# A four-stage transformer-like kernel: sine tables in paced pieces, bias adds and last weights placed late, ones set by VectorE

## The reference

```python
x = x + tanh(g_xattn[0]) * mamba(ctx_1024, layernorm(x))       # selective scan
x = x + tanh(g_ffn[0])   * moe(layernorm(x))                   # 16 experts, top 2, plus a shared one
x = x + tanh(g_xattn[1]) * attention(layernorm(x), ctx_1024)   # below
x = x + tanh(g_ffn[1])   * ffn(layernorm(x))                   # ternary weights, int8-like rows

# attention: 32 heads of 16, queries from x, keys and values from the context
q, k = axial_rope(x @ Wq, pos), axial_rope(ctx @ Wk, pos)      # cos and sin of pos * freq
w = softmax(q @ k.T / 4)
out = (w @ (ctx @ Wv)) @ Wout + bout
# ffn: w_q = clip(round(w / rms(w)), -1, 1) * rms(w);  x_q = round(x * 127 / max|x|)
out = bitlinear(gelu(bitlinear(x, w1)), w2)
```

## Time and profile before

| what | value |
|---|---|
| median of 3 runs | 1558.94 us |
| lowest and highest | 1556.22 and 1568.86 us |
| the profiled execution's own time | 1561.57 us |
| its span, first to last instruction | 1559.7 us |
| mean granted TensorE clock in it | 0.964 of full speed |
| busy: TensorE, VectorE, ScalarE, GpSimd | 1431.7, 1110.9, 998.1, 657.7 us |

### The profile page before, as it was taken

How to read it: one execution, slowest core, us unless ns; L and a number is a source line. 1 busy time by engine, 2 the same in 40 slices (tenths; PEclk the granted TensorE clock), 3 DMA queues, 4 the chain that set the end, 5 groups by cost and what they waited for, 6 DMA issues and landing times. The chain is left out here.

```text
span 1559.7 us, 20801 instructions
## 1 busy us (share of the span) xinstructions
PE 1431.7 (92%) x6056; PEld 613.8 (39%) x6057; DVE 1110.9 (71%) x1628; ACT 998.1 (64%) x1544; POOL 657.7 (42%) x440
## 2 busy tenths in 40 slices
PE   6688988988988979999999899699999999999999
PEld 2344434434444424444444344123333333244444
DVE  7999999999996422222222488889999999647985
ACT  3999998999974003323233154478788788877764
POOL 0689799698986530056656565240000000000000
PEclk7799999999999989999999999699999999999999
DMA  5212314113205374779963566352322322220464
GB/s 189 68 52 83 95 55 121 42 56 109 75 15 197 141 143 108 195 194 247 313 175 95 196 202 163 101 182 75 96 74 73 95 76 73 61 108 14 88 142 122
DMA packets 181164, 183.46 MB, mean 118 GB/s; under 512 B 104564, under 2 KB 132596, under 8 KB 180324
## 3 DMA queue, kind: packets, MB, share of 16 engines
q1 hardware_dynamic: 113846, 123.83, 27.8%
q0 software_dynamic: 9472, 33.89, 7.6%
q10 hardware_dynamic: 57776, 24.89, 6.6%
HBM read 96.97 MB, written 54.92 MB: 97 GB/s over the span
## 5 line engine op out<-in xcount | busy, mean ns | idle before, releaser
L1924 DVE TENSOR_REDUCE a_mx<-a_s 128x2 f32<-128x1024 f32 x256 | 303.2, 1218 | 35.3 <-PE a_s L2041 32.4
L284 POOL TENSOR_TENSOR m_hs<-m_hs,m_C 128x1024 f32<-128x1024 f32 x128 | 301.6, 2376 | 54.3 <-DVE m_hs L509 53.5
L509 DVE TENSOR_TENSOR_SCAN m_hs<-m_dA,m_d 128x512 f32<-128x512 f32 x256 | 294.6, 1201 | 11.8 <-PE m_d L664 10.8
L1376 PE MATMUL e_gu<-e_w,e_xgT 128*128 x376 | 171.0, 598 | 5.9 <-issue 5.9
L664 PE MATMUL m_d<-ident_sb,m_dBuT 128*128 128x128 f32 x1024 | 160.7, 291 | 16.6 <-DVE m_hs L509 9.9
L390 ACT ACTIVATE m_dA<-m_dt,m_negA 128x512 f32<-128x512 f32 x256 | 167.9, 711 | 11.2 <-DMA m_dt<-m_dt 10.6
L664 PEld LDWEIGHTS m_d<-ident_sb,m_dBuT 128*128 128x128 f32 x1024 | 118.0, 146 | 141.0 <-DVE m_hs L509 72.0
L368 ACT ACTIVATE m_dBuT<-m_dtuT,m_BT 128x512 f32<-128x512 f32 x241 | 157.8, 711 | 0.4 <-PE m_d L664 0.3
L2041 PE MATMUL a_s<-ring_sb 96*128 96x512 bf16 x512 | 152.3, 390 | 5.9 <-DVE a_mx L1924 4.0
L679 PE MATMUL m_y<-m_hs,m_fold 128*64 128x512 f32 x512 | 142.2, 636 | 3.7 <-POOL m_hs L284 3.7
L2315 POOL MEMSET f_ones<- 128x128 f32 x1 | 0.2, 204 | 343.3 <-POOLq L1508 343.3
(11 more groups left out here) (350 smaller groups left out, 2404.3 us busy)
## 6 DMA issues: line engine op xcount, KB each, us to landing
e_w<-in_ex_gu SPq DMA_DIRECT2D x16, 1024.0 KB, 7.9
ring_sb<-qk_dram SPq DMA_DIRECT2D x64, 192.0 KB, 3.2
xg_dram<-zeros_sb SPq DMA_DIRECT2D x47, 256.0 KB, 3.1
yg_dram<-attn_sb ACTq DMA_DIRECT2D x47, 256.0 KB, 3.6
m_C<-c_dram SPq DMA_DIRECT2D x64, 128.0 KB, 2.9
m_dt<-m_dt SPq DMA_DIRECT2D x64, 128.0 KB, 2.4
e_w<-in_ex_dn SPq DMA_DIRECT2D x16, 512.0 KB, 9.9
ring_sb<-qk_dram SPq DMA_DIRECT2D x64, 128.0 KB, 3.2
```

Source lines behind the costliest of these rows:

```text
L284: pool.tensor_tensor(hs[:, J % RH], hs[:, J % RH], C2[:, N % RC].unsqueeze(1).broadcast_to([P, 2, L]), ALU.mult).then_inc(s_hc, 1)
L509: dve.tensor_tensor_scan(hs[:, J % RH, h], dA[:, j % RA], pd[j % RD][:], 0.0, ALU.mult, ALU.add)\
L1376: last = pe.matmul(pgu[par][:], lhs(k), rhs(k), start=(k == 0), stop=(k == KD - 1))
L1924: dve.tensor_reduce(mx[:, r % 2, h * TB + 2 * c:h * TB + 2 * c + 2], psc[c][:], AX.X, ALU.max)\
```

## The change

Four edits, each to where or when something is done; what is computed stays the same.

1. In `moe`, the 8 table loads no longer stand together behind the scatter. Load q waits for `s_y` = NT + 1 + q, and they are issued between the early loads, two behind each of the first four. The wait for all tables comes behind the first seven early loads, ahead of the first key rows.
2. In `attention`, GpSimd's 16 additions of the bias wait for the last split of maxima (`s_n` = 4 * NG).
3. The load of `w1` leaves GpSimd's queue. SyncE issues it in four pieces of 1 MB, one at the end of its part of each of the last four steps; SyncE waits for all stored parts between the first four steps and the loop. ScalarE waits for four pieces.
4. The memset of the ones in `vout` goes from GpSimd's to VectorE's queue, first in both.

```diff
--- before.py
+++ after.py
@@ -973,9 +973,6 @@
             pool.wait_ge(s_sct, 16 * 2 * NT)
             pool.wait_ge(s_tst, 16)
             pool.sem_inc(s_kd, 2)
-            for q in range(HALF):
-                pool.dma_start(tab[q * HD:(q + 1) * HD], tab_dram[:, q, :].partition_broadcast(HD)).then_inc(s_tab, 16)
-            pool.wait_ge(s_y, NT)
             at = {"ctxT": 0, "wv": KC * T, "wk": KC * T + KC * D, "wq": KC * T + 2 * KC * D}
 
             def load_early(n, name, k, width, col=0):
@@ -984,6 +981,10 @@
                     pool.wait_ge(s_early, 16 * n)
                 to = at[name] + k * (T if name == "ctxT" else D) + col
                 pool.dma_start(early[:, to:to + width], a[name][k * P:(k + 1) * P, col:col + width]).then_inc(s_early, 16)
+
+            def load_table(q):
+                pool.wait_ge(s_y, NT + 1 + q)
+                pool.dma_start(tab[q * HD:(q + 1) * HD], tab_dram[:, q, :].partition_broadcast(HD)).then_inc(s_tab, 16)
 
             EARLY = [("wk", k, D) for k in range(KC)] + [("ctxT", k, L, b * L) for b in range(B) for k in range(KC)] + \
                 [("wv", k, D) for k in range(KC)] + [("wq", k, D) for k in range(KD)]
@@ -1014,11 +1015,15 @@
                     dst = qk_dram[1, m, :, c * HALF:(c + 1) * HALF].rearrange("a d h t -> (d h) a t")
                     pool.dma_start(dst, kparts[:, c]).then_inc(s_kst, 16)
 
-            pool.wait_ge(s_tab, 16 * HALF)
             for m in range(2 * B):
                 first = 0 if m == 0 else KEYS_FROM + 2 * m
                 for n in range(first, min(KEYS_FROM + 2 * m + 2, len(EARLY))):
                     load_early(n, *EARLY[n])
+                    if m == 0:
+                        for q in range(2 * n, min(2 * n + 2, HALF)):
+                            load_table(q)
+                if m == 0:
+                    pool.wait_ge(s_tab, 16 * HALF)
                 key_rows(m)
             pool.wait_ge(s_kst, 32 * 2 * B)
 
@@ -1680,6 +1685,12 @@
                 if inside(i, r + 1):
                     load_v(i, r + 1)
                     maxima(i, r + 1)
+                if isinstance(i, int) and i == NG // RG - 1:
+                    sp.dma_start(w1[:, r], a["w1T"][r * P:(r + 1) * P]).then_inc(s_last, 16)
+
+            def parts_stored():
+                for r in range(RP):
+                    sp.wait_ge(s_ps[r], 32 * ITEMS // RP)
 
             for b in range(B):
                 sp.wait_ge(s_vc, TB * (b + 1))
@@ -1705,14 +1716,13 @@
             for n in range(ITEMS - 2, ITEMS):
                 store(n)
 
-            run(sp, step)
+            run(sp, step, parts_stored)
             sp.wait_ge(s_t, 16 * (NG - 2))
             sp.dma_start(flat[:, half // 2:half // 2 + KD * D].rearrange("p (k e) -> p k e", k=KD),
                          a["wo"].rearrange("(k p) e -> p k e", p=P)).then_inc(s_wo, 16)
 
         @block.gpsimd
         def _(pool):
-            pool.memset(vout.rearrange("p r g t (h c) -> p (r g t h) c", h=G4)[:, :, HD:VW], 1.0).then_inc(s_vone, 1)
             pool.wait_ge(s_yst[0], 16 * (ST - ST // 2))
             pool.wait_ge(s_yst[1], 16 * (ST // 2))
             def inverse_root(b):
@@ -1753,13 +1763,11 @@
                 part_3(n - 1)
             part_3(ITEMS - 1)
             pool.dma_start(bo[:], a["bo"].partition_broadcast(P)).then_inc(s_bo, 16)
-            for r in range(RP):
-                pool.wait_ge(s_ps[r], 32 * ITEMS // RP)
-            pool.dma_start(w1[:], a["w1T"].rearrange("(k p) e -> p k e", p=P)).then_inc(s_last, 16)
             pool.wait_ge(s_bo, 16)
             pool.tensor_scalar(bo[:], bo[:], g_out, None, ALU.mult).then_inc(s_bg, 1)
             pool.wait_ge(s_bg, 1)
             pool.wait_ge(s_xn, NT)
+            pool.wait_ge(s_n, 4 * NG)
             for t in range(NT):
                 pool.tensor_tensor(x_sb[:, t], x_sb[:, t], bo[:], ALU.add).then_inc(s_xb, 1)
 
@@ -1874,6 +1882,7 @@
 
         @block.vector
         def _(dve):
+            dve.memset(vout.rearrange("p r g t (h c) -> p (r g t h) c", h=G4)[:, :, HD:VW], 1.0).then_inc(s_vone, 1)
             dve.memset(m3[:], 0.0).then_inc(s_zero, 1)
 
             def combine(t):
@@ -2324,11 +2333,11 @@
 
         @block.scalar
         def _(act):
-            weights = ((w1[:], w1q, s_w), (w2, w2q[:], s_w2))
+            weights = ((w1[:], w1q, s_w, 16 * KD), (w2, w2q[:], s_w2, 16))
 
             def square(n):
-                w, wq, loaded = weights[n]
-                act.wait_ge(loaded, 16)
+                w, wq, loaded, count = weights[n]
+                act.wait_ge(loaded, count)
                 act.activation(wq, w, ACT.Square, accum_out=ssq[:, n:n + 1]).then_inc(s_sq, 1)
 
             def weight_std(n):
@@ -2336,7 +2345,7 @@
                 act.activation(sd[:, n:n + 1], sd[:, n:n + 1], ACT.Sqrt).then_inc(s_sd, 1)
 
             def round_weight(n):
-                w, wq, loaded = weights[n]
+                w, wq = weights[n][:2]
                 act.wait_ge(s_k, 2 * n + 2)
                 act.wait_ge(s_c, 3)
                 act.activation(w, w, ACT.Identity, scale=rms[:, n:n + 1], bias=magic[:, 0:1]).then_inc(s_q, 1)
```

## The result

| | before | after |
|---|---|---|
| median, us | 1564.57 (1556.09 to 1569.64, 20 runs) | 1553.57 (1547.98 to 1566.45, 20 runs) |
| ratio to before, 95% interval | 1 | 0.9935 [0.9918, 0.9952] |
| span of the profiled execution, us | 1559.7 | 1551.6 |

The change takes 0.65% off, some 10 us (the ratio is taken over all runs; that of the two medians is 0.9930); the forecast was 0.73%, 11.3 us. The median of 1553.57 lies above the 1547.6 forecast mainly because before itself, in the twenty runs beside it, has a median of 1564.57 and not the 1558.94 of the three shown.

The account below looks back on a forecast made before the run. TensorE was taken to bound the kernel nearly throughout, with VectorE in the attention loop. The terms -7.5 + 1.0 - 4.8 + 0.2 - 0.2 sum to -11.3 us, forecasting 1547.6 us, range 1542 to 1555.

Parts of the forecast that it names:

- Tables: Behind the scatter: without the table burst, TensorE's 5.89 us stall and 1.57 us of slow products go, -7.5 us.
- The signs named for this part: At the first routed tile: transposes land under 7 us, no TensorE gap before it, eight first products in 3.6 us.
- The stall has no other owner: Behind the scatter: without the tables, turned rows arrive by 570, before TensorE's work ends at 578.32; 5.89 us of standing goes.
- Pieces: Routed experts: paced table pieces may delay turned rows near the first weight reload by up to 2.2 us each; +1.0 us.
- rival A: First transposed loads stay slow for another reason, such as two blocking each other; only -5 us, 1554 us; 12%.
- One sign of being wrong: Routed experts: ScalarE waits over 2 us for turned rows within the first ten tiles.
- Rival C: Slower: paced pieces fill the DMA engines beside the expert reload; 15.6 us lost against 12.5 gained, 1562 us; 5%.
- Additions and weights: Early attention loop: moving the bias additions and the 4 MB weight load away gives -4.8 us, bounds 2 and 5.3.
- Rival B: Long early attention steps belong to the loop's start, not to additions and weights; only -6.5 us, 1552.5 us; 12%.
- Weights late: End of attention: four pieces on SyncE's queue stay hidden, output weights land between 1365 and 1370; +0.2 us, bounds 0 and 1.5.
- additions at the end: Behind the last split: the sixteen additions end near 1371.3, covered by some 5 us; cost 0, bounds 0 to 1.
- Ones: Ahead of the gathers: memset moved to VectorE frees GpSimd's queue, gathers at most 0.8 us earlier; -0.2 us.

Follow-up runs that it names:

- e1: The kernel before with only the sine tables loaded in paced pieces; 1547.43 us, ratio 0.9926 to before.
- e6: The changed kernel itself, unaltered, run again beside the others; 1546.65 us, ratio 0.9918 to before.
- e5: The changed kernel with the eight table pieces started four tiles earlier, four of them ahead of the early loads; 1542.35 us, ratio 0.9900 to before.
- e9: The changed kernel with table pieces four tiles earlier and without the sixteen bias additions (output lacks the out bias); 1542.03 us, ratio 0.9892 to before.
- e4: The changed kernel with the tables loaded in one burst behind the scatter again; 1554.62 us, ratio 0.9965 to before.
- e2: The kernel before with only the sixteen bias additions moved behind the last split of maxima; 1556.16 us, ratio 0.9980 to before.
- e7: The changed kernel with all eight table pieces issued at once behind the first routed tile; 1554.36 us, ratio 0.9962 to before.
- e10: The changed kernel with table pieces four tiles earlier and the sixteen additions released at the 16th split of maxima; 1550.67 us, ratio 0.9938 to before.

## Why the prediction was right

**Tables, forecast -7.5.** The place, the owner and the size in the pair of profiles held: 6.4 us less from scatter to first routed product (26.48 to 20.05), and behind it 1.57 less for eight products. The signs named for this part came: first rows in 3.00 us, no gap, 3.60 us. What I mis-sized is what the burst costs in a usual execution. "The stall has no other owner" was true, but I took its 5.88 us for its price; it was the part of 11 us that the standstill of ScalarE and TensorE during the scatter had not already covered. A second profile of a kernel with the burst would have shown it.

**Pieces, forecast +1.0, bounds 0 and 7.** Measured: 2.0 us of gaps in after, 1.5 in e1, and in e6 two gaps of 4.4 and 4.3 us and a slow clock. Against e5's 286.6 us from the first routed product to attention that is 3.2 us in after, 2.6 in e1 and 14 in e6. The value was near in after, but the upper bound was too low. I priced a piece by what it takes of the DMA engines, 2.2 us, and looked at turned rows only. Two things were left out: the store of results, on ScalarE's queue behind the transposed load with only two buffers, and the issue itself, which beside the pieces held that queue for up to 3.06 us in after, 4.11 in e1 and 7.72 in e6. My rival A had named such an issue (the 10.97 us above), and I put no price on it. One sign of being wrong came just outside its bounds: ScalarE waits 3.77 us for the turned rows of the twelfth tile, at 636.45. Rival C, given 5%, named such a case by sum (15.6 us) with the wrong first victim; the one profile of this size is of the slowest of e6's six executions.

**Additions and weights, forecast -4.8, bounds 2 and 5.3.** Measured -4.48 in the five steps. Rival B is refuted: with both gone the steps are at 59.31 us, so the start of the loop has no excess of its own beyond the 12.36 us of its first step, which stays. My base of 11.69 a step was 0.17 too low as a mean of five (59.31 / 5 = 11.86), which is the 0.8 us between my excess of 5.3 and the true 4.48.

**Weights late, +0.2, and additions at the end, 0.** Both hidden: the seam is 27.36 us beside 27.37. e9 shows it for the additions. The clock behind the seam, +1.3 us, was in no step of mine.

**Ones, -0.2.** Nothing: VectorE's memset takes 0.38 us at 869.30, the first gather starts 0.76 us behind TensorE's first product instead of 1.03, and from there to the third split it is 132.08 us beside 131.93.

In the profiles the stages sum to -6.4 us from the scatter to the first routed product, 0 from there to attention (the 1.57 us of clock regained and what the pieces cost cancel), +0.2 to the third split, -4.5 in the five steps, 0 at the seam and +1.3 in the last stage, -9.4 together; the last scatter issue is 1.3 us later in after, which makes the 8.1 us between the spans. So two terms were a little off and one was missing, and they nearly cancelled. By the median of 20 runs it is -11.0 us beside a forecast of -11.3, closer than the steps deserve, and in part luck: e1 alone gives -11.5 and e4 -5.5 us, 17 together, and the whole 10 to 13. With two executions of one kernel 11 us apart from the first routed product to attention (289.8 and 300.7), I leave that sum unexplained.

## What to carry to other kernels

A gap of one execution can be less than what its cause costs, if the engine came late to it for another reason; look at what delayed it just before. Before pacing a transfer into a stretch, list every transfer whose issue or buffer stands on the same queue as the critical one, not only the critical one. The cheapest place tried here is the one ahead of the reload, four tiles earlier (e5, 1542.35 us, the fastest version that computes everything). A long run of GpSimd additions has a price that depends on where a short VectorE operation meets it (0, 5.2 or 11.65 us for the same sixteen), so it belongs behind the last such operation.

## What the runs showed of the hardware

- The issue of a transposed load on ScalarE's queue takes 1.25 us undisturbed, up to 3.06, 4.11 and 7.72 us beside the pieces (after, e1, e6) and 5.22, 10.97 or 12.68 us beside a burst of tables (e2, before, e7). What stands behind it on that queue starts after it: the sigmoid of e2 at 585.99, that of e6 at 625.37.
- A VectorE operation that takes 0.17 us elsewhere took 9.01 us beside back-to-back GpSimd additions of 1.23 us each, and ended with the last of them (e10).
- ScalarE stood for 28.72 us in before and 28.98 us in after while the indirect scatters ran, ahead of anything that was changed, and TensorE paused with it (4.9 us in four pauses, and 4.54 us at 550.73). The other ten profiles lack it, e6 of the same kernel among them. The releaser is one that the profile calls remote. The one transfer of instructions that the profile has in that stretch (queue q8, 16 KB) starts at 549.2 us in before and 556.5 in after, in the ten others between 540.8 and 546.4. Whether that is cause or consequence no run tells.
- The same pause of 2.3 us in the last stage was followed by the lower clock in e9 (sixteen products in 5.30 us) and not in e10 (3.63 us).
